# Conditioned residual layer on one core: loads split over queues by halves of SBUF, the bias made in columns, five product banks

## What is computed

```python
hidden = concatenate([cond, cond], axis=-1)              # 4 x 512
x_mean = mean(x, axis=1, keepdims=True)                  # 4 x 1 x 512
fused  = concatenate([x, x_mean * ones_L, hidden[:, None, :] * ones_L], axis=-1)
out    = x + relu(einsum('bld,do->blo', fused, W) + b)
```

## Time and profile before

| Engine | busy, us | share of the span |
|---|---|---|
| PE | 105.0 | 89% |
| DVE | 87.0 | 73% |
| ACT | 48.2 | 41% |
| POOL | 46.7 | 39% |

### The profile page before, as it was taken

The page is one execution under the profiler, slowest core; times in us unless marked ns, Lnnn a source line. Parts: engine busy times, 40 slices in busy tenths (PEclk is TensorE's granted clock), DMA queues, the critical chain, the costliest instruction groups (busy, mean ns, idle before and its releaser), DMA issues.

```text
span 118.5 us, 1775 instructions
## 1 busy us (share of the span) xinstructions
PE 105.0 (89%) x490; PEld 82.7 (70%) x490; DVE 87.0 (73%) x163; ACT 48.2 (41%) x118; POOL 46.7 (39%) x46
## 2 busy tenths in 40 slices
PE   5948999953999989997999999999999999999910
PEld 2308998831458868875888888778888887999900
DVE  1017849880179799999999996399999997897640
ACT  4039416900023998004956700067486001833310
POOL 6329401016000000069966750045856439992000
PEclk9997699996579999999999999999999999999996
DMA  2999999999999999993594928600068194297996
GB/s 87 228 218 225 217 200 225 346 280 211 216 213 211 213 212 206 209 213 69 124 224 105 217 47 189 165 0 0 0 145 206 43 214 100 56 216 167 220 235 177
DMA packets 35975, 20.28 MB, mean 171 GB/s; under 512 B 1920, under 2 KB 34688, under 8 KB 35968
## 3 DMA queue, kind: packets, MB, share of 16 engines
q1 hardware_dynamic: 34528, 18.88, 77.8%
q10 hardware_dynamic: 1248, 0.79, 2.4%
q0 software_dynamic: 192, 0.52, 2.1%
HBM read 11.80 MB, written 8.39 MB: 170 GB/s over the span
## 4 chain that ended last, share of the span: by engine, by line
PE 48%; SPq 13%; DVE 13%; DMA 12%; ACT 5%; issue 4%; ACTq 0%
PE ps_y L409 47%; DMA xa<-in_x_dram 12%; SPq L161 5%; DVE ps_xt L299 3%; SPq L140 3%; ACT xh L235 3%; ACT relu_t L255 3%; DVE back L316 2%; SPq L170 2%; DVE w2x L333 2%; DVE bias_row L347 2%; PE ps_mean L427 1%; DVE xl L305 1%; SPq L168 1%; DVE const_row L375 1%
## 5 line engine op out<-in xcount | busy, mean ns | idle before, releaser
L409 PE MATMUL ps_y<-xh,w1h 128*128 128x256 f32 (+2 forms) x160 | 55.0, 370 | 3.4 <-ACT xh L235 2.3
L205 POOL TENSOR_TENSOR xa<-xa,back 128x512 f32 x28 | 36.0, 1305 | 42.9 <-DVE back L316 42.9
L409 PE MATMUL ps_y<-xl,w1h 128*128 128x256 f32 (+2 forms) x160 | 52.4, 354 | 0.0
L409 PE MATMUL ps_y<-xh,w1l 128*128 (+2 forms) x144 | 50.3, 366 | 0.0
L409 PEld LDWEIGHTS ps_y<-xh,w1h 128*128 128x128 f32 x160 | 29.5, 197 | 10.3 <-issue 3.6
L255 ACT ACTIVATE relu_t<-ps_y,bias 128x512 f32<-128x512 f32 (+1 forms) x32 | 20.0, 634 | 32.9 <-DVE bias L350 25.5
L299 DVE STREAM_TRANSPOSE ps_xt<-xa 128x512 f32<-128x512 f32 (+1 forms) x36 | 22.3, 641 | 14.6 <-DMA xa<-in_x_dram 14.3
L409 PEld LDWEIGHTS ps_y<-xl,w1h 128*128 128x128 f32 x160 | 29.6, 197 | 4.8 <-issue 1.2
L235 ACT ACTIVATE xh<-ps_xt 128x512 fp32r<-128x512 f32 (+1 forms) x36 | 19.8, 550 | 26.4 <-DVE ps_xt L299 26.0
L409 PEld LDWEIGHTS ps_y<-xh,w1l 128*128 128x128 f32 x144 | 27.1, 189 | 4.4
L305 DVE TENSOR_TENSOR xl<-ps_xt,xh 128x512 fp32r<-128x512 f32 (+1 forms) x36 | 22.2, 617 | 4.2 <-ACT xh L235 4.2
(11 more groups left out here) (21 smaller groups left out, 22.6 us busy)
## 6 DMA issues: line engine op xcount, KB each, us to landing
xa<-in_x_dram SPq DMA_DIRECT2D x28, 256.0 KB, 6.8
out_dram<-xa SPq DMA_DIRECT2D x28, 256.0 KB, 3.9
xa<-in_x_dram SPq DMA_DIRECT2D x8, 128.0 KB, 6.6
w<-in_L_cond_W_dram SPq DMA_DIRECT2D x4, 256.0 KB, 7.1
w<-in_L_cond_W_dram SPq DMA_DIRECT2D x2, 512.0 KB, 9.9
w<-in_L_cond_W_dram POOLq DMA_DIRECT2D x4, 128.0 KB, 5.5
out_dram<-xa SPq DMA_DIRECT2D x4, 128.0 KB, 3.0
out_dram<-xa ACTq DMA_DIRECT2D x4, 128.0 KB, 2.9
```

Source lines behind the costliest of these rows:

```text
L205: nc.gpsimd.tensor_tensor(rows, rows, back[:, t], ALU.add).then_inc(added, 1)
L409: return nc.tensor.matmul(ps_y[:, t, ls], lhs, rhs, start=start, stop=stop, skip_group_check=True)
```

## The change

All these parts are made together:

- **Loads.** The first half of group 0, W1 and the second half of group 0 are issued by SP for the quadrants 0 and 1 and by ACT for 2 and 3. W1 comes in parts of k = 0, k = 1 and k = 2, 3 instead of two halves. Of group 1 and W2 SP issues quadrants 0 and 1, and POOL 2 and 3, once the first half of group 0 has landed. POOL and ACT issued parts of W1 before. All later groups of x are issued by SP in the order of quadrants 0, 2, 1, 3, with no wait between them; every group has a semaphore of its own.
- **Bias in columns.** POOL copies W2 into a tiled order (`w2t`, four copies) and adds the halves of W3 in two pieces in tiled order. PE makes the constant by eight matmuls with four columns, and the mean by four with one column, so the bias comes out with one output feature per partition. DVE then needs one small instruction per batch, and one more for the constant. b is loaded in columns by four transfers of single words, in place of one of 256 KB to all partitions. cond is no longer spread.
- **First mean.** DVE weighs each k of W2 as soon as that piece of group 1 is done, not after all four.
- **PSUM.** Constant and mean share one bank, and `ps_y` has five banks. Only tiles 0 and 1 are saved.
- **W1's rounding** is shared: ACT rounds k = 0 and 2, DVE k = 1 and 3.
- **Group 0 on PE.** The first half gets all three products before the second half begins.
- **Order of x on DVE and ACT.** Transposes stand two pieces ahead; the bias of the second group of a batch is summed behind tile 0 of it.
- WARM, the matmuls that only warm PE, are 13 instead of 14. Loops over registers are written out.

The core of the diff:

```diff
-Y_BANKS = 4
+Y_BANKS = 5
+SAVED = 2
-WARM = 14
+WARM = 13
+EVEN, ODD = (0, 1), (2, 3)
...
         @block.sync
-            load_x0(sp, 0)
-            load_w1(sp, 1, range(0, 2), w1_landed)
-            load_x0(sp, 1)
-            load_x(1, 1)
-            sp.dma_start(cond_c[:], cv).then_inc(cond_landed, 16)
-            for j in range(NQ):
-                sp.dma_start(w2[Q * j:Q * j + Q], wv[1, j]).then_inc(w2_landed, 16)
+            load_x0(sp, 0, EVEN)
+            for part in range(3):
+                load_w1(sp, part, EVEN)
+            load_x0(sp, 1, EVEN)
+            load_x(sp, 1, EVEN, x_landed[1])
+            load_w2(sp, EVEN, w2_landed)
             for r in range(2):
                 sp.dma_start(w3[:, r], w3v[r]).then_inc(w3_landed, 16)
-            sp.dma_start(b_row[:], bvec.partition_broadcast(P)).then_inc(b_landed, 16)
-            load_x(2, 0)
-            with sp.Fori(1, B - 1) as b:
-                sp.wait_ge(x_landed[1], 16 * NQ * b)
-                load_x(H * b + 1, 1)
...
+            for g in range(2, G):
+                load_x(sp, g, (0, 2, 1, 3), x_landed[g])
...
         @block.gpsimd
+            pool.wait_ge(x0_landed[0], 16 * NQ)
+            load_x(pool, 1, ODD, x1_odd_landed)
+            load_w2(pool, ODD, w2_odd_landed)
...
+            for k in range(NK):
+                nc.gpsimd.tensor_copy(as_tiles(w2t[:, k]), by_tile(w2[:, k])).then_inc(w2_tiled, 1)
             pool.wait_ge(w3_landed, 16 * 2)
-            nc.gpsimd.tensor_tensor(w3sum[:], w3[:, 0], w3[:, 1], ALU.add).then_inc(w3_added, 1)
+            for k in range(CK):
+                nc.gpsimd.tensor_tensor(as_tiles(w3sum[:, k]), by_tile(w3[:, 0, k]), by_tile(w3[:, 1, k]),
+                                        ALU.add).then_inc(w3_added, 1)
...
         @block.tensor
+            def const_terms():
+                pe.wait_ge(cond_landed, 16)
+                pe.wait_ge(w3_added, CK)
+                for t in range(NK):
+                    for k in range(CK):
+                        nc.tensor.matmul(ps_const[:, t], w3sum[:, k, t], cond_c[:, :, k],
+                                         start=(k == 0), stop=(k == CK - 1))
             def mean_bias(b):
                 pe.wait_ge(w2x_step, NK * b + NK)
-                nc.tensor.matmul(ps_mean[:], ones[:], w2x[:], start=True, stop=True).then_inc(mean_done, 1)
+                for t in range(NK):
+                    last = nc.tensor.matmul(ps_mean[:, t:t + 1], w2x[:, t], ones[:], start=True, stop=True)
+                last.then_inc(mean_done, 1)
```

394 lines of the change are left out of this document (192 added, 202 removed).

## The result

The changed kernel takes 122.45 us (median of 6 runs, 121.34 to 123.79), the kernel before 120.59 in the same session. The ratio is 1.0135, 95% interval 1.008 to 1.0189: slower by about 1.3%, where 116.5 us had been forecast. The profiled execution has a span of 120.6 us and took 122.82.

The account below looks back on a forecast made before the run. PE was taken as the bound from its restart at 34.0 us, with a waiting start before it. Span 118.5 - 3.2 (restart) - 1.1 (idle) + 0.3 (later means) = 114.5, plus 2.0 outside: 116.5 us; range 110.0 to 120.5.

Parts of the forecast that it names:

- The frame: Whole kernel: what the start gains is gained at the end; time is 85.7 us plus the effective restart.
- effective restart: When PE runs on without waiting, behind the constant, mean and slow matmul: 30.8 us forecast against 34.0, 3.2 us gained.
- The idle time from 40 to 60 us: PE's waits there, 1.1 us, taken as gained through the fifth bank, fewer saved tiles and less DVE work.
- a later mean: Means of later batches on PE: eight loads, 0.96 us against 0.86 each, 0.3 us lost over three.
- Early rate: Loads at the start: 290 GB/s for the first 2.1 MB, with SP and ACT each serving one half of SBUF.
- Landing of W2: Loads: 4.2 MB at 290, then 226 GB/s, bring W2 by 19.8 us.
- POOL's work behind W2: POOL: four copies, 4.0 us, then W3's sum, 2.4; W3 lands at 22.4, hidden; PE's constant starts at 26.2 us.
- rival D: POOL's four transfers take 10.8 us of its own time, so the constant starts at 29.5: 119.8 us; chance 12%.
- At nothing: WARM 13, early weighing, W1's rounding on DVE and group 0's split priced at zero; DVE through the mean about 22 us.
- Small matmuls: Constant and first mean on PE as 24 narrow instructions: 4.0 us, between 2.9 and 8.1, against 4.47 before.
- the slow matmul behind: First wide matmul on PE after the narrow ones: 0.6 us extra, between nothing and the 0.96 seen before.
- The rivals: Halves add fully, 110.6 us (20%); halves add nothing, 118.6 to 119.7 (17%); rival D (12%); rest, DVE delaying PE (5%).

Follow-up runs that it names:

- e10: Changed kernel with first-mean weighings behind all of group 1, filling matmuls before constant and mean, and SP alone issuing group 1 and W2: 118.8 us.
- e7: Changed kernel with group 1 and W2 all issued by SP, in quadrant order 0, 2, 1, 3, none by POOL: 120.49 us.
- e14: e13 with group 1 and W2 issued by SP alone, in quadrant order 0, 2, 1, 3: 116.71 us.
- e3: Changed kernel with DVE's weighings of W2 behind all pieces of group 1, as in the kernel before: 119.89 us, ratio to before 0.9862.
- e1: Changed kernel with 19 dummy matmuls on PE in the pauses of tile 4: 119.13 us, ratio to before 0.9852.
- e9: Kernel before with 8 filling matmuls on PE ahead of the constant: 121.51 us, ratio to before 1.0114.
- e16: Changed kernel with weighings behind all of group 1, filling matmuls before constant and mean, four product banks instead of five, four tiles saved: 121.39 us.
- e13: Changed kernel with weighings behind all of group 1, constant and mean behind tile 5, three tiles saved, no fill: 117.79 us, ratio to before 0.9711.

## Why the prediction was wrong, step by step

**The frame held.** "time = 85.7 us + the effective restart" gives, in terms of the span, 118.5 + 3.5 (restart 37.5 against 34.0) - 1.1 - 0.2 = 120.7 us, against 120.6 measured. The idle time from 40 to 60 us is gone, as said, and a later mean costs 0.79 us, less than the 0.96 put in. What failed is the restart: 30.8 forecast, 37.5 measured. Of the 6.7 us, 3.9 lie ahead of the constant (30.11 against 26.2: POOL had the sum of W3 ready at 29.15, which is 2.95 of it, and DVE's delay of tile 4 adds 0.96) and 2.8 in and behind the small matmuls.

**Early rate: right.** 290 GB/s forecast for SP and ACT together; 288 measured from 2 to 5 us, and 278 from 2 to 10 us, with POOL's transfers issued from 4.89 on. The kernel before, with its own queues, in the same stretch (no PE column):

```profile
2.00:10.00 8.00, 1.00 1.09 228
```

The Trainium skill, "SBUF — State Buffer", section "Can I just issue two DMAs to hit both halves?", would have two transfers to the two halves at 6% above one; the traces disagree where SP and ACT share: 278 is 31% above the 213 of the earlier trace rows and 22% above this 228. For SP alone, alternating between halves, they do not decide: 229 and 232 from 10 to 16 us in e10 and e7, 8 to 9% above 213, but 286 in e14.

**"Landing of W2", 19.8: failed, 21.86.** The sum of bytes was right, but not whose bytes. POOL's halves landed 8.0 and 9.4 us after they were issued, SP's half of W2 13.5, and at the end only one half was still on its way, at 185 GB/s from 16 to 20 us. Transfers of after by kind (number, size, median us from issue to landing):

```profile
xa<-in_x_dram POOLq DMA_DIRECT2D x2, 256.0 KB, 8.0
w<-in_L_cond_W_dram POOLq DMA_DIRECT2D x2, 256.0 KB, 9.4
w<-in_L_cond_W_dram SPq DMA_DIRECT2D x2, 256.0 KB, 13.5
```

A block is there when its later half is. All nine traces with these loads have W2 at 20.25 or later (e10), so this step failed in each of them, not only in the one profiled here. It counted two queues as one stream.

**"POOL's work behind W2": half right.** Four copies took 2.47 us, not 4.0, and the four transfers 2.57 (1.46 + 1.11), which rules rival D out. W3 was to be there at 22.4 and hide behind the copies; it came at 26.17, no earlier than before, and its sum took 2.98. By itself this gives 29.15 for the constant, not 26.2, and later than the 28.60 of before: in this run the gain was already gone here. The bytes say how: up to 26 us this run had moved 221 GB/s on average and the kernel before 225. What it was ahead by 10 us it lost again at 185 from 16 to 20 us and at 198 from 22 to 26, where the kernel before sent W3 at 388. That W3 stands in SP's queue behind the late half of W2 fits this; why the rate stayed so low was not tested. This run is a late one, too: over the nine traces the middle value for W3 is 24.76, while the four of the kernel before and its variants have 26.11, 24.42, 26.27 and 26.50.

**"At nothing": the step that failed most.** By the experiments it is the dearest: undone (e3) or filled (e1), it gives back 2.7 to 2.8%. In the sum of this run it shows directly with only 0.96 us, since POOL's sum ended at 29.15; the rest comes through the clock and through what differs between the runs, and no run parts the two. I had DVE through with the mean at 22 us. It was through at 30.0, and it, not POOL, released PE (28.67, behind the subtraction of 27.94). Three things were missing from that sum, and a fourth was mis-sized without effect. Group 1 landed at 18.49, after 3.33 us of waiting. The weighings stand between the pieces of x, so a wait for W2 delayed tile 4, which needs no mean. A weighing beside POOL's sum of W3 took 1.60 instead of 0.75 us. And the two roundings took 1.76 and 1.47 us instead of 0.73, beside POOL's subtractions, which kept their 1.28; but DVE then waited 3.33 us for group 1 anyway, so this did not reach the mean. In e7, where the subtraction began 0.66 us ahead of the cast, the cast took 0.90. The first pair of the changed kernel, then of e7:

```profile
7.36 1.76 DVE L280 CAST w1h<-w 128x512 fp32r<-128x512 f32 x1
7.54 1.29 POOL L181 TENSOR_TENSOR w1l<-w,w1h 128x512 fp32r<-128x512 f32 x1
7.37 0.90 DVE L281 CAST w1h<-w 128x512 fp32r<-128x512 f32 x1
6.71 1.28 POOL L182 TENSOR_TENSOR w1l<-w,w1h 128x512 fp32r<-128x512 f32 x1 [6.27 <-ACT w1h L212]
```

Both casts end 0.3 us behind the end of the subtraction (9.12 behind 8.83, 8.27 behind 7.99), and so do all 26 casts of the thirteen traces that have them: the cast is held until the subtraction is over. The 0.90 of e7 is therefore no price of a cast alone either. On these last two the Trainium skill, "SBUF — State Buffer", section "Who interferes with whom", has a DVE instruction with two inputs in SBUF contend with GpSimd's reads, and a cast in a two-port mode and a GpSimd instruction shut each other out whole, whichever is issued first. The traces agree on the whole block, if the cast runs in such a mode, which no trace shows. They do not agree on the order as their starts show it: the cast of 7.36 started ahead of the subtraction of 7.54, and was the one that waited (POOL was issuing a transfer until 7.44). I had named that rule in the one direction that did not occur, DVE blocking POOL, and put no price on it.

**"Small matmuls", 4.0, and "the slow matmul behind", 0.6: failed together.** I asked what narrow matmuls cost, and took 4.0 for 4.98. The larger part is what they do to the clock. At full clock they cost 2.7 to 2.8 us (e1, e14), under the lower bound I had put, at half 4.98, and behind them 12 wide matmuls still went at half: 2.44 us against 0.6. In the kernel before, three wide float32 matmuls stood there, and the clock was back after one slow matmul behind them. In the sum: 1.0 + 1.8 = 2.8 us.

**The rivals.** None of them names what happened. The price of rival D, a late constant, is close to it (29.5), but its cause was absent. What I had left out is that a change can keep PE as busy as before and lower its clock. I saw 0.58 in the earlier trace rows and counted it as a thing of before that the change would take along.

**A hidden limit of the frame.** In the kernel before, the restart was worth less than I thought: below 33.6 us (34.0 less 0.39) the relus bind, as e9 shows. The changed kernel does not have that second bound. The bank is part of the reason (e16: 0.94 us of idle ahead of tile 8 without it); the bias in columns should be the other part, but no run has it alone. The same kind of fill makes the kernel before slower by 1.1% (e9) and takes the changed one from 1.35% slower to 1.5% faster (e1). The change has more room and a worse start; e13 and e14 keep the room and mend the start.

## What to carry to other kernels

Price a replaced matmul twice: by its own time, and by what the granted clock is behind it; where short matmuls stand next to a pause, put real dense work between them and the pause (e13: 4.2% below the changed kernel, though the clock still fell for about 3 us). A block split over queues lands with its slower half, so count the landing of the block and of what is queued behind it, not the GB/s, and look at several runs: W3 landed anywhere in 3.5 us with the same loads. Before trusting "everything gained at the start is gained at the end", look how far behind the bound the next wait is: 0.39 us was all there was, and an experiment that only moves the first bound shows it.
